# Graph attention: the closing sums of a block dealt out over five source tiles, the negated features one tile behind their low halves

## The chip, the cores and the metric

The kernel runs on one core of one Trainium2 chip. The metric is device microseconds of one execution. Three runs of the kernel before took 1197.7, 1198.29 and 1210.78 us; their median, 1198.29 us, is the time before.

## The reference, cut to what matters

A graph of 3125 nodes (64 features) and 100000 edges goes through four residual layers, each followed by a layer norm: ten rounds of normalized neighbour sums, an edge-feature layer with batch norm, two rounds of neighbour sums with two linear maps, and a four-headed graph attention. Only the last is touched here:

```python
logits = leaky_relu(a_src[src] + a_dst[dst], 0.2)        # per edge (self loops added), per head
ex     = exp(logits - seg_max[dst])
alpha  = ex / (segment_sum(ex, dst)[dst] + 1e-16)
out    = segment_sum(x[src] * alpha[:, :, None], dst).mean(heads) + bias
x      = layernorm(x + out)
```

## The kernel before, in words

Early stages turn the edge list into a dense count matrix `C` in SBUF (f16, 25 source tiles of 128 nodes by 3200 target columns) and run the first three layers as matmuls against it. In attention no exponential is taken per edge. Because the leaky ReLU has two slopes, an edge's weight is one of two products of a source factor and a target factor, and which one holds depends only on whether the logit is positive. So per head, source tile and target column the kernel needs a 0/1 step, times the count.

The stage runs over 4 heads (`h`), 5 blocks of 5 target tiles (`b`, 640 columns) and 25 source tiles (`t`); one (h, b, t) is called a unit here. In a unit:

- ScalarE (ACT, line 966) writes the step of 128x640 into `Mr`, a ring of 6 slots, with a sigmoid of a very steep slope. It waits until TensorE is done with the unit six earlier (`s_Mu`).
- VectorE (DVE, line 1587) multiplies it by the counts and signals `s_M`. For a few units per block (`STT`, line 1597) DVE makes the step itself.
- TensorE (PE) runs five matmuls `Mr` by `F` (line 2141, 260 columns: features for both slopes, each as a high and a low f16 half) and five matmuls of the plain counts by `FN` (line 2137, 130 columns: the negated features of the other slope). For some units (`SPLIT`) the plain matmuls are replaced by a complement that DVE makes (`Nr`, line 1550) and PE uses one unit later (line 2207). The plain matmuls of the first two target tiles of a block are sent ahead of the block ("lead").

Two kinds of work are threaded between the units on DVE and ACT by hand-written tests on `t`:

- **Features.** For each head and each group of 5 source tiles, PE makes `x` times the head's weight (`xw`), DVE scales it into `Vx` (`scaled`, line 1471), ACT rounds the high half into `F` (`high_f`, line 907; waits for `Vx`), DVE makes the low half (`low_f`, line 1487; waits for `s_fhi`) and, behind a wait on that, the negated copy `FN` (line 1489), which signals `s_F`. PE waits on `s_F` at the head's block 0: for the first three groups at once in heads 1 to 3, and ahead of the first unit of each later group. In head 0 all of this lies in block 0. For the later heads three groups are made in block 4 of the head before and two in block 0 of the head itself.
- **Closing sums.** At t = 4 of the next block ACT and DVE take a finished block from PSUM (lines 942 and 1496). At t = 5 `post` (lines 1502 to 1510) runs five DVE operations, each waiting for the one before: join the halves, denominator, reciprocal, product, add to `acc`. It signals `s_post`, which ACT waits for at t = 4 of the block after (`take`) and the first step of `final` waits for. In the last head `final` (lines 1518 to 1539) runs the layer norm of the block before in six steps at t = 8, 10, 12, 14, 16, 18, and signals `s_fin`, for which SP sends the rows out.

`c` counts DVE operations on a semaphore; `c.here()` is a wait of DVE for all that it has counted. SP's queue stores the target scores to DRAM (line 577) and then, in the branch of this path, waits for that store (`s_rowsout`) and loads each block's scores back, broadcast over partitions, one block ahead (line 604).

Of the kernel before, what the change touches and what calls it, by code (L numbers as in the profile page):

```python
# [4 lines left out]
ALU = mybir.AluOpType  # L5
# [7 lines left out]
P = 128  # L13
LO = 2048.0
# [24 lines left out]
def gnn_kernel(nc, x, dst, edges, We, be, W1, b1, gamma, beta, W2, b2, Wl, bl, Wr, br, Wg, att_s, att_d, bias_g, out):  # L39
    N, D = out.shape  # L40
# [15 lines left out]
    H = att_s.shape[1]  # L56
# [6 lines left out]
    XS = 256.0  # L63
    S1 = D + 1
# [7 lines left out]
    NG = 5  # L72
    NT = T // NG
# [25 lines left out]
    with ExitStack() as ctx:  # L99
# [102 lines left out]
        acc = xs  # L202
# [165 lines left out]
        def pairs_of(t0):  # L368

            return F[:, t0:t0 + NT, :].rearrange("p t (e l c) -> p (t e) l c", e=2, l=2)  # L370
# [141 lines left out]
        def _(sp):  # L512
# [62 lines left out]
                general_hop(kk, kk % 2)  # L575
            sp.wait_ge(s_minusrow, 1)
            sp.dma_start(minus_dram.rearrange("h (t p) -> (h t) p", p=P), minus_row[:]).then_inc(s_rowsout, 16)
            sp.wait_ge(s_flag3, 1)
            dense3 = sp.value_load(flag[0:1, 1:2], min_val=0, max_val=1)
            with sp.If(dense3 == 0):  # L580
# [13 lines left out]
                        sp.dma_start(g_raw[0:GE, :], edges[bass.ds(ch * GE, GE), :]).then_inc(g_load3, 16)  # L594
            with sp.Else():

                sp.wait_ge(s_rowsout, 16)
                for blk in range(1, H * NG):
                    if blk >= 2:
                        sp.wait_ge(s_M, (blk - 1) * T)  # L600
                    else:
                        sp.wait_ge(s_whl, 1)
                    b_ = blk % NG
                    sp.dma_start(nadS[blk % 2], minus_dram[blk // NG:blk // NG + 1, b_ * NG * P:(b_ + 1) * NG * P].to_broadcast([P, NG * P])).then_inc(s_nadl[blk % 2], 16)
# [114 lines left out]
        def _(act):  # L719
# [180 lines left out]
            def high_f(h, g):  # L900

                gi = h * NG + g
                t0 = g * NT
                act.wait_ge(s_vx, gi + 1)
                if h:
                    act.wait_ge(s_Mu, unit(h - 1, NG - 1, t0 + NT - 1) + 1)
                act.activation(pairs_of(t0)[:, :, 0, :], Vx[gi % 2].rearrange("p t e c -> p (t e) c"), ACT.Copy, scale=1.0 / LO).then_inc(s_fhi, 1)  # L907
# [26 lines left out]
            with act.If(dense3 == 1):  # L934

                def take(h, b):

                    act.wait_ge(s_Mu, unit(h, b, T - 1) + 1)
                    act.wait_ge(s_post, h * NG + b)
                    for j in range(NT):  # L940
                        t = b * NT + j
                        act.activation(r1[:, j], bank[:, BANKS[b][j], 0:2 * S1], ACT.Identity, scale=ex[:, 1, h, t:t + 1]).then_inc(s_c2, 1)

                for h in range(H):
                    for b in range(NG):
                        blk = h * NG + b
                        if blk:
                            act.wait_ge(s_nadl[blk % 2], 16 * ((blk + 1) // 2))
                        else:
                            act.wait_ge(s_nads, 1)  # L950
                        for t in range(T):
                            mi = unit(h, b, t)
                            if t == 4 and blk:
                                take((blk - 1) // NG, (blk - 1) % NG)
                            if blk == 0 and t in (1, 6, 11, 16):
                                high_f(0, (t + 4) // 5)
                            if blk and b == 0 and t in (9, 16):
                                high_f(h, 3 + t // 16)
                            if b == NG - 1 and h < H - 1 and t in (11, 16, 21):
                                high_f(h + 1, (t - 11) // 5)  # L960
                            if by_act(h, b, t):
                                if mi >= RB:
                                    act.wait_ge(s_Mu, mi - RB + 1)
                                    if unit_of(mi - RB) in APART:
                                        act.wait_ge(s_N, APART[unit_of(mi - RB)] + 1)
                                act.activation(Mr[:, mi % RB, :], nadS[blk % 2], ACT.Sigmoid, bias=steep[:, h, t:t + 1], scale=-STEEP / XS).then_inc(s_step, 1)  # L966
                act.activation(small[0:1, 63:64], onesP[0:1, :], ACT.Sqrt)
                act.wait_ge(s_post, H * NG - 1)
                for j in range(NT):
                    t = (NG - 1) * NT + j  # L970
                    act.wait_ge(s_Mu, unit(H - 1, NG - 1, T - LATE) + j + 1)
                    act.activation(r1[:, j], bank[:, BANKS[NG - 1][j], 0:2 * S1], ACT.Identity, scale=ex[:, 1, H - 1, t:t + 1]).then_inc(s_c2, 1)
                for part_, (a_, z_) in enumerate(((0, FRONT), (FRONT, NT))):
                    act.wait_ge(s_var, 3 * NB + part_ + 1)
                    act.activation(sd[:, a_:z_], mv[:, a_:z_, 1], ACT.Sqrt, bias=eps_c[:]).then_inc(s_sd, 1)
                act.wait_ge(s_rs, NB + 1)
                for j in range(FRONT):
                    t = (NG - 1) * NT + j
                    last = act.activation(acc[:, t, :], acc[:, t, :], ACT.Identity, bias=small[:, 40 + j:41 + j], scale=small[:, 32 + j:33 + j])
                last.then_inc(s_fin, 1)  # L980
# [11 lines left out]
        def _(v):  # L992
# [487 lines left out]
            with v.If(dense3 == 1):  # L1480

                def low_f(h, g):

                    gi = h * NG + g
                    t0 = g * NT
                    v.wait_ge(s_fhi, gi + 1)
                    c.add(v.scalar_tensor_tensor(pairs_of(t0)[:, :, 1, :], pairs_of(t0)[:, :, 0, :], -LO, Vx[gi % 2].rearrange("p t e c -> p (t e) c"), ALU.mult, ALU.add))  # L1487
                    c.here()
                    v.tensor_scalar(FN[:, t0:t0 + NT, :], F[:, t0:t0 + NT, 2 * S1:4 * S1], -1.0, None, ALU.mult).then_inc(s_F, 1)  # L1489

                def evicted(h, b):

# [2 lines left out]
                        v.wait_ge(s_c2, TURN[h, b, j] + 1)  # L1495
                        v.scalar_tensor_tensor(r1[:, j], bank[:, BANKS[b][j], 2 * S1:4 * S1], ex[:, 3, h, t:t + 1], r1[:, j], ALU.mult, ALU.add).then_inc(s_ring, 1)

                def post(h, b):

                    t0 = b * NT  # L1500
                    v.wait_ge(s_ring, TURN[h, b, NT - 1] + 1)
                    c.add(v.scalar_tensor_tensor(q, r1[:, :, S1:2 * S1], 1.0 / LO, r1[:, :, 0:S1], ALU.mult, ALU.add))
                    c.here()
                    c.add(v.tensor_scalar(rd[:], q[:, :, D], 1e-16 * XS, float(H), ALU.add, ALU.mult))
                    c.here()
                    c.add(v.reciprocal(rd[:], rd[:]))
                    c.here()
                    c.add(v.tensor_tensor(q[:, :, 0:D], q[:, :, 0:D], rd[:, :, None].to_broadcast([P, NT, D]), ALU.mult))
                    c.here()
                    v.tensor_tensor(acc[:, t0:t0 + NT, :], acc[:, t0:t0 + NT, :], q[:, :, 0:D], ALU.add).then_inc(s_post, 1)  # L1510

                def final(b, step):

# [36 lines left out]
                    v.tensor_tensor(Nr[ni % RN], Mr[:, unit(h, b, t) % RB, :], C[:, t, b * NT * P:(b + 1) * NT * P], ALU.subtract).then_inc(s_N, 1)  # L1550

                low_f(0, 0)
                scaled(0, 1)
                v.wait_ge(s_self, NB)
                for h in range(H):
                    for b in range(NG):
                        blk = h * NG + b
                        for t in range(T):
                            mi = unit(h, b, t)
                            if t == 4 and blk:  # L1560
                                evicted((blk - 1) // NG, (blk - 1) % NG)
                            if t == 5 and blk:
                                post((blk - 1) // NG, (blk - 1) % NG)
                            if blk == 0:
                                if t in (5, 10, 15):
                                    scaled(0, (t + 5) // 5)
                                elif t in (2, 7, 12, 17):
                                    low_f(0, (t + 3) // 5)
                            elif b == 0:
                                if t in (8, 15):  # L1570
                                    scaled(h, 2 + t // 7)
                                elif t in (11, 18):
                                    low_f(h, 2 + t // 9)
                            if b == NG - 2 and h < H - 1 and t in (10, 15):
                                scaled(h + 1, (t - 10) // 5)
                            if b == NG - 1 and h < H - 1:
                                if t == 14:
                                    scaled(h + 1, 2)
                                elif t in (12, 17, 22):
                                    low_f(h + 1, (t - 12) // 5)  # L1580
                            if h == 0 and b == 0 and t == 14:
                                c.add(v.tensor_tensor(acc[:], acc[:], biases[:, 2:3, :].to_broadcast([P, T, D]), ALU.add))
                            if h == H - 1 and b >= 1 and t in (8, 10, 12, 14, 16, 18):
                                final(b - 1, (t - 8) // 2)
                            if by_act(h, b, t):
                                v.wait_ge(s_step, steps(h, b, t))
                                v.tensor_tensor(Mr[:, mi % RB, :], Mr[:, mi % RB, :], C[:, t, b * NT * P:(b + 1) * NT * P], ALU.mult).then_inc(s_M, 1)  # L1587
# [699 lines left out]
```

## Time and profile before

| | us |
|---|---|
| median of the runs | 1198.29 |
| the profiled execution, its time | 1197.28 |
| its span, first to last instruction | 1195.4 |
| PE busy in the span | 1082.5 (91%) |
| DVE busy | 863.9 (72%) |
| ACT busy | 628.7 (53%) |
| line 2141, PE matmuls of steps by features | 321.2 |
| line 2137, PE matmuls of counts by negated features | 187.3 |
| line 1587, DVE products of steps and counts | 207.6 |

The page of the profile has the busy time of each engine, the span in 40 slices, the chain of work that ended last, and the costliest groups of instructions with the idle time before them. Attention fills the slices from the 26th on: there PE stands at 9 tenths or more, DVE and ACT at 9, and PE's granted clock at 9 tenths or more of full speed. Idle time is put down to what ended it.

### The profile page before, as it was taken

How to read it: one execution, taken by the hardware profiler on the slowest of the kernel's cores; microseconds unless marked ns; L12 is line 12 of the kernel's file. 1: busy time of each engine (PE TensorE's matmuls, PEld its weight loads, DVE VectorE, ACT ScalarE, POOL GpSimd, SP SyncE). 2: the span in 40 equal slices, each digit the busy share in tenths (PEclk: the TensorE clock that was granted, in tenths of full speed). 3: DMA queues.
4: the chain of work that ended last, by engine and by line, in shares of the span. 5: the costliest groups of instructions: out<-in, count | busy, mean ns of one | idle time of the engine just before them, and what ended most of it. 6: DMA issues, size and time to landing. Idle time of an engine off the chain costs nothing.

```text
span 1195.4 us, 38826 instructions
## 1 busy us (share of the span) xinstructions
PE 1082.5 (91%) x15999; PEld 997.2 (83%) x15999; DVE 863.9 (72%) x2311; ACT 628.7 (53%) x1172; POOL 59.6 (5%) x106
## 2 busy tenths in 40 slices
PE   4877777779999999999998999599999999999997
PEld 3766666669999999999973999489989988998996
DVE  5999999975444444444562544789999999999997
ACT  2777777730000000000111402579989999998997
POOL 1000000001111111111000011000000000000000
PEclk7899999989999999999999799699999999999999
DMA  5555555510000000000000000000000000000010
GB/s 80 69 78 77 72 74 73 71 39 3 2 3 2 3 2 3 2 2 3 2 2 1 2 2 2 15 12 13 24 12 24 13 24 13 24 13 20 16 29 14
DMA packets 135931, 28.04 MB, mean 23 GB/s; under 512 B 132609, under 2 KB 133093, under 8 KB 135778
## 3 DMA queue, kind: packets, MB, share of 16 engines
q1 hardware_dynamic: 132816, 25.25, 12.9%
q8 instruction: 116, 1.90, 0.7%
q10 hardware_dynamic: 2962, 0.58, 0.3%
q14 instruction: 37, 0.30, 0.1%
HBM read 24.97 MB, written 0.85 MB: 22 GB/s over the span
## 4 chain that ended last, share of the span: by engine, by line
PE 63%; DVE 12%; ACT 3%; issue 2%; ACTq 0%; POOL 0%; DVEq 0%
PE bank L2018 33%; PE bank L2141 13%; PE bank L2137 6%; DVE Mr L1587 4%; PE bank L1955 3%; PE bank L2207 2%; PE bank L1947 2%; ACT Mr L966 1%; DVE F L1487 1%; PE bank L1982 1%; PE bank L1939 1%; ACT F L907 1%; PE bank L2040 1%; DVE Mr L1597 1%; DVE FN L1489 0%
## 5 line engine op out<-in xcount | busy, mean ns | idle before, releaser
L2018 PE MATMUL bank<-GH,C 128*128 128x128 f16 x7100 | 397.7, 219 | 0.0
L2018 PEld LDWEIGHTS bank<-GH,C 128*128 128x128 f16 x7100 | 396.9, 98 | 0.1
L2141 PE MATMUL bank<-F,Mr 128*128 128x260 f16 (+1 forms) x2538 | 321.2, 261 | 10.0 <-DVE Mr L1587 8.7
L2141 PEld LDWEIGHTS bank<-F,Mr 128*128 128x128 f16 x2538 | 213.2, 98 | 33.7 <-DVE Mr L1587 11.0
L1587 DVE TENSOR_TENSOR Mr<-Mr,C 128x640 f16<-128x640 f16 x461 | 207.6, 485 | 25.4 <-ACT Mr L966 24.3
L814 ACT ACTIVATE plo<-bank 128x256 f32<-128x256 f32 (+1 forms) x84 | 30.1, 360 | 364.3 <-PE bank L2018 346.0
L2137 PE MATMUL bank<-FN,C 128*128 128x130 f16 x1945 | 187.3, 220 | 0.0
L1234 DVE TENSOR_TENSOR S<-bank,plo 128x256 f32<-128x256 f32 (+1 forms) x84 | 33.2, 395 | 212.9 <-ACT plo L814 212.8
L1810 PE MATMUL bank<-ohk,ohp 128*128 128x100 f16 (+3 forms) x1452 | 115.9, 216 | 69.6 <-ACT C L756 35.1
L966 ACT ACTIVATE Mr<-cold,eaT 128x640 f16<-128x640 f32 x231 | 172.4, 819 | 8.1 <-PE bank L2141 7.7
L966 ACT ACTIVATE Mr<-eaT 128x640 f16<-128x640 f32 x230 | 171.7, 818 | 7.3 <-PE bank L2141 7.0
L1810 PEld LDWEIGHTS bank<-ohk,ohp 128*128 128x128 f16 x1452 | 88.4, 101 | 79.2 <-ACT C L756 45.5
L2137 PEld LDWEIGHTS bank<-FN,C 128*128 128x128 f16 x1945 | 138.0, 98 | 4.9
L756 ACT ACTIVATE C<-bank 128x325 f32 (+1 forms) x242 | 111.0, 459 | 58.9 <-PE bank L1820 52.6
L1066 DVE TENSOR_TENSOR ohk<-iota_key,key 128x904 f16<-128x904 f16 (+7 forms) x264 | 106.5, 473 | 0.0
L1820 PEld LDWEIGHTS bank<-ohj,eahl 128*65 128x65 f16 x968 | 71.6, 117 | 11.1
L1825 PE MATMUL bank<-C,spare 128*128 (+1 forms) x242 | 79.1, 328 | 0.2 <-ACT C L756 0.2
L1068 DVE TENSOR_TENSOR ohp<-iota_p,pl 128x2048 f16<-128x2048 f16 (+1 forms) x66 | 75.2, 1139 | 0.0
L1820 PE MATMUL bank<-ohj,eahl 128*65 128x6 f16 x968 | 66.9, 177 | 0.0
L646 POOL TENSOR_TENSOR xc<-xs,cold 128x256 f32<-128x256 f32 (+1 forms) x63 | 40.3, 645 | 520.0 <-DVE V L1250 267.2
L1121 DVE SCALAR_TENSOR_TENSOR GH<-GH,V 128x256 f16<-128x256 f16 (+1 forms) x84 | 47.1, 561 | 2.9
L1056 DVE TENSOR_TENSOR raw<-raw,eahl 128x768 f32<-128x768 f32 (+1 forms) x44 | 39.4, 895 | 3.0 <-ACT eahl L745 3.0
(271 smaller groups left out, 984.4 us busy)
## 6 DMA issues: line engine op xcount, KB each, us to landing
raw<-in_edges_dram SPq DMA_DIRECT2D x237, 68.0 KB, 2.5
cold<-minus_dram SPq DMA_DIRECT2D x10, 320.0 KB, 3.3
eaT<-minus_dram SPq DMA_DIRECT2D x9, 320.0 KB, 3.5
xs<-in_x_dram SPq DMA_DIRECT2D x1, 800.0 KB, 4.4
out_dram<-xs SPq DMA_DIRECT2D x4, 160.0 KB
raw<-in_edges_dram ACTq DMA_DIRECT2D x5, 68.0 KB, 3.2
dsts<-in_dst_dram SPq DMA_DIRECT2D x1, 240.0 KB
dsts<-in_dst_dram ACTq DMA_DIRECT2D x1, 180.0 KB
```

The source lines that it names most:

```text
L756: act.activation(C[:, :, bass.ds(wi * W, W)], pk[w % RING][:, 0:KEY].rearrange("p (j t) -> p t j", t=T), ACT.Copy).then_inc(s_evict, 1)
L966: act.activation(Mr[:, mi % RB, :], nadS[blk % 2], ACT.Sigmoid, bias=steep[:, h, t:t + 1], scale=-STEEP / XS).then_inc(s_step, 1)
L1066: v.tensor_tensor(ohk[:, o:o + n, OK[k]:OK[k + 1]].rearrange("p w (n e) -> p w n e", e=2), pairs(iota_key[:, OK[k]:OK[k + 1]], n), key2[:, ...
L1068: v.tensor_tensor(ohp[:, o:o + n].rearrange("p w k (n e) -> p (w k) n e", e=2), pairs(iota_p[:], n * K), pl2[:, par, w0:w1_].rearrange("p ...
L1121: last = v.scalar_tensor_tensor(GH[:, par, t0:t0 + n, D:2 * D], GH[:, par, t0:t0 + n, 0:D], -LO, src, ALU.mult, ALU.add)
L1587: v.tensor_tensor(Mr[:, mi % RB, :], Mr[:, mi % RB, :], C[:, t, b * NT * P:(b + 1) * NT * P], ALU.mult).then_inc(s_M, 1)
L1810: pe.matmul(pk[r][:, T * j0:T * j1], ohp[:, o, k], ohk[:, o, a_:a_ + T * (j1 - j0)], start=q_ == 0, stop=q_ == len(PART) - 1)
L1820: last = pe.matmul(pea[par][0:65, w * W + j0:w * W + j1], eahl[:, ch, :], ohj[:, par, j0:j1, ch], start=False, stop=w == WG - 1 and k == K ...
L1825: return pe.matmul(pdeg[:, 0:KEY].rearrange("p (t j) -> p t j", j=W), ident16, C[:, :, bass.ds(wi * W, W)], start=False, stop=stop)
L2018: last = pe.matmul(bank[:, b, jj * 2 * D:(jj + 1) * 2 * D], C[:, t, (t0 + jj) * P:(t0 + jj + 1) * P], GH[:, par, t, :], start=t == 0 and j ...
L2137: pe.matmul(bank[:, k, 2 * S1:4 * S1], C[:, t, t_ * P:(t_ + 1) * P], FN[:, t, :], start=start, stop=False)
L2141: return pe.matmul(bank[:, k, a_:z_], Mr[:, mi % RB, j * P:(j + 1) * P], F[:, t, a_:z_], start=start, stop=t == T - 1)
```

## The change

SP's wait for its store of the target scores is moved ahead of the read of the branch flag. ACT's `high_f` calls of block 0 are moved to later `t`. On DVE, `FN` leaves `low_f` and becomes `plain_f`, called one source tile later, with its 650 elements walked in the order (half, tile, column), rows of 65, where they were walked (tile, column), rows of 130. `post` is cut into five calls, one at each of t = 5 to 9. Some `low_f` calls and all steps of `final` are moved to later `t`. PE's code is untouched.

```diff
@@ sync
             sp.dma_start(minus_dram..., minus_row[:]).then_inc(s_rowsout, 16)
+            sp.wait_ge(s_rowsout, 16)
             sp.wait_ge(s_flag3, 1)
...
-                sp.wait_ge(s_rowsout, 16)
@@ scalar
-                            if blk == 0 and t in (1, 6, 11, 16):
+                            if blk == 0 and t in (1, 8, 13, 18):
                                 high_f(0, (t + 4) // 5)
-                            if blk and b == 0 and t in (9, 16):
-                                high_f(h, 3 + t // 16)
+                            if blk and b == 0 and t in (11, 18):
+                                high_f(h, 3 + t // 18)
@@ vector
                     c.add(v.scalar_tensor_tensor(pairs_of(t0)[:, :, 1, :], ..., -LO, Vx[...], ALU.mult, ALU.add))
+
+                def plain_f(g):
+
+                    t0 = g * NT
                     c.here()
-                    v.tensor_scalar(FN[:, t0:t0 + NT, :], F[:, t0:t0 + NT, 2 * S1:4 * S1], -1.0, None, ALU.mult).then_inc(s_F, 1)
+                    v.tensor_scalar(FN[:, t0:t0 + NT, :].rearrange("p t (l c) -> p l t c", l=2), F[:, t0:t0 + NT, 2 * S1:4 * S1].rearrange("p t (l c) -> p l t c", l=2), -1.0, None, ALU.mult).then_inc(s_F, 1)
...
-                def post(h, b):
+                def post(h, b, step):
...
                 low_f(0, 0)
+                plain_f(0)
                 scaled(0, 1)
...
-                            if t == 5 and blk:
-                                post((blk - 1) // NG, (blk - 1) % NG)
+                            if 5 <= t < 10 and blk:
+                                post((blk - 1) // NG, (blk - 1) % NG, t - 5)
                             if blk == 0:
                                 if t in (5, 10, 15):
                                     scaled(0, (t + 5) // 5)
-                                elif t in (2, 7, 12, 17):
+                                elif t in (2, 8, 13, 18):
                                     low_f(0, (t + 3) // 5)
+                                elif t in (3, 9, 14, 19):
+                                    plain_f((t + 2) // 5)
                             elif b == 0:
                                 if t in (8, 15):
                                     scaled(h, 2 + t // 7)
-                                elif t in (11, 18):
+                                elif t in (12, 18):
                                     low_f(h, 2 + t // 9)
+                                elif t in (13, 19):
+                                    plain_f(2 + t // 9)
...
                                 elif t in (12, 17, 22):
                                     low_f(h + 1, (t - 12) // 5)
+                                elif t in (13, 18, 23):
+                                    plain_f((t - 13) // 5)
...
-                            if h == H - 1 and b >= 1 and t in (8, 10, 12, 14, 16, 18):
-                                final(b - 1, (t - 8) // 2)
+                            if h == H - 1 and b >= 1 and t in (10, 12, 14, 16, 18, 20):
+                                final(b - 1, (t - 10) // 2)
```

## Rows read from the trace of the kernel before

**Rows 1.** Waits from 770 us on: us in total, times, longest us.

```profile
DVE Mr L1587 <- ACT Mr L966: 24.3, 62, 1.1
...
PE bank L2141 <- DVE Mr L1587: 8.7, 16, 2.7
```

**Rows 2.** Windows: stretch, its us, busy us (instructions) by engine, PEclk, DMA share, GB/s.

```profile
800.30:880.00 79.70, 79.08 (x1049) 73.35 (x1047) 74.03 (x176) 74.62 (x115) 0.00 (x0) 1.00 0.06 15
1104.00:1124.00 20.00, 19.86 (x254) 18.24 (x253) 19.11 (x68) 19.00 (x30) 0.00 (x0) 1.00 0.05 18
```

**Rows 3.** Timeline, head 0, block 0: start us, us, engine, line, form, [idle before].

```profile
787.27 1.82 DVE L1582 TENSOR_TENSOR xs<-xs,cold 128x1600 f32<-128x1600 f32 x1
787.86 0.72 PE L2141 MATMUL bank<-F,Mr 128*128 128x260 f16 x5
...
793.99 0.73 PE L2141 MATMUL bank<-F,Mr 128*128 128x260 f16 x5 [0.66 <-DVE Mr L1587]
...
796.51 0.72 PE L2141 MATMUL bank<-F,Mr 128*128 128x260 f16 x5
```

**Rows 4.** Timeline, head 0, block 4: DVE's second feature group, then PE's units.

```profile
871.83 0.83 DVE L1487 SCALAR_TENSOR_TENSOR F<-F,eaT 128x650 f16<-128x650 f16 x1
872.69 0.49 DVE L1489 TENSOR_SCALAR FN<-F 128x650 f16<-128x650 f16 x1
873.10 1.29 DVE L1587 TENSOR_TENSOR Mr<-Mr,C 128x640 f16<-128x640 f16 x3
...
871.84 0.72 PE L2141 MATMUL bank<-F,Mr 128*128 128x260 f16 x5
872.56 0.72 PE L2141 MATMUL bank<-F,Mr 128*128 128x260 f16 x5
873.64 0.73 PE L2141 MATMUL bank<-F,Mr 128*128 128x260 f16 x5 [0.19 <-DVE Mr L1587]
876.39 0.72 PE L2141 MATMUL bank<-F,Mr 128*128 128x260 f16 x5
877.71 0.73 PE L2141 MATMUL bank<-F,Mr 128*128 128x260 f16 x5 [0.43 <-DVE Mr L1587]
```

**Rows 5.** Timeline, head 1, block 0, around its last feature group.

```profile
891.64 0.83 DVE L1471 TENSOR_TENSOR Vx<-bank,ex 128x650 f32<-128x650 f32 x1
892.39 0.48 DVE L1587 TENSOR_TENSOR Mr<-Mr,C 128x640 f16<-128x640 f16 x1
892.51 0.76 ACT L907 ACTIVATE F<-Vx 128x650 f16<-128x650 f32 x1 [0.99 <-DVE Vx L1471]
893.37 0.72 PE L2141 MATMUL bank<-F,Mr 128*128 128x260 f16 x5
894.56 0.73 PE L2141 MATMUL bank<-F,Mr 128*128 128x260 f16 x5 [0.19 <-DVE Mr L1587]
896.95 0.73 PE L2141 MATMUL bank<-F,Mr 128*128 128x260 f16 x5 [0.54 <-DVE Mr L1587]
```

**Rows 6.** Timeline, head 3, block 1: DVE's closing sums.

```profile
1107.92 0.49 DVE L1502 SCALAR_TENSOR_TENSOR wts<-r 128x325 f32<-128x325 f32 x1
1108.45 0.17 DVE L1504 TENSOR_SCALAR rd<-wts 128x5 f32<-128x5 f32 x1
...
1109.40 0.49 DVE L1510 TENSOR_TENSOR xs<-xs,wts 128x320 f32<-128x320 f32 x1
```

**Rows 7.** Timeline, the last block: PE's weight loads for its last unit.

```profile
1183.72 0.56 PEld L2141 LDWEIGHTS bank<-F,Mr 128*128 128x128 f16 x6 [0.30 <-DVE Mr L1587]
```

**Rows 8.** Groups by line and form from 770 us on: count, busy us, mean ns, idle before.

```profile
L1489 DVE TENSOR_SCALAR FN<-F 128x650 f16<-128x650 f16 x20 | 9.9, 493 | 0.7
L1487 DVE SCALAR_TENSOR_TENSOR F<-F,eaT 128x650 f16<-128x650 f16 x10 | 8.3, 829 | 0.8 <-ACT F L907 0.8
```

**Rows 9.** Timeline, SP's queue: the store of the scores, the first load back.

```profile
769.18 0.34 SPq L577 DMA_DIRECT2D minus_dram<-minus_row  x1
770.73 0.35 SPq L604 DMA_DIRECT2D cold<-minus_dram  x1
```

More of the change, by code:

```diff
@@ L1496, in evicted @@
                         v.scalar_tensor_tensor(r1[:, j], bank[:, BANKS[b][j], 2 * S1:4 * S1], ex[:, 3, h, t:t + 1], r1[:, j], ALU.mult, ALU.add).then_inc(s_ring, 1)
-                def post(h, b):
+                def post(h, b, step):
                     t0 = b * NT
[L1501 to L1510, printed above, removed]
+                    if step == 0:
+                        v.wait_ge(s_ring, TURN[h, b, NT - 1] + 1)
+                        c.add(v.scalar_tensor_tensor(q, r1[:, :, S1:2 * S1], 1.0 / LO, r1[:, :, 0:S1], ALU.mult, ALU.add))
+                    elif step == 1:
+                        c.here()
+                        c.add(v.tensor_scalar(rd[:], q[:, :, D], 1e-16 * XS, float(H), ALU.add, ALU.mult))
+                    elif step == 2:
+                        c.here()
+                        c.add(v.reciprocal(rd[:], rd[:]))
+                    elif step == 3:
+                        c.here()
+                        c.add(v.tensor_tensor(q[:, :, 0:D], q[:, :, 0:D], rd[:, :, None].to_broadcast([P, NT, D]), ALU.mult))
+                    else:
+                        c.here()
+                        v.tensor_tensor(acc[:, t0:t0 + NT, :], acc[:, t0:t0 + NT, :], q[:, :, 0:D], ALU.add).then_inc(s_post, 1)
                 def final(b, step):
```

## The prediction

> **What bounds the kernel now.** I read the windows first, to find where attention is held; then the waits of that stretch by engine; then the timeline of PE, DVE and ACT around each wait; then the groups for durations. In the stretch from 800 to 880 us PE is busy for 79.08 of 79.70 us at full granted clock, with DVE and ACT at 74 [rows 2]: three engines nearly level, PE the bound. What DVE can still give back is PE's wait for a step times counts. These waits are 16, 8.7 us in all [rows 1]. The longest, 2.7 us, is the first unit of the stage, which this change leaves alone; the others are three in the first block and four at each of the three changes of head. That DVE in its turn waits 62 times for ACT, 24.3 us in all, says that DVE is not always the late one.
>
> The idle time that a row gives in brackets understates the loss, because a matmul's end is modelled; I count from start to start. In block 0 the units from 793.99 to 796.51 us come every 0.84 us, but four units take 6.13 us from 787.86 to 793.99 [rows 3]: 2.77 us lost. In block 4 of head 0 the pace is 0.72 us; two units come 0.36 and 0.60 us later than that (873.64 and 877.71) [rows 4]. In block 0 of head 1 the pace is 0.84 again; the two starts at 894.56 and 896.95 us lose 0.35 and, over two units, 0.71 us [rows 5]. The last two patterns stand three times.
>
> **What causes them.** In block 4 DVE makes a low half and, chained to it, the negated copy, 0.86 + 0.41 us, in front of one product for which PE is already waiting [rows 4]. In block 0 of head 1 ACT asks for the high half's input at t = 16 and stands 0.99 us until DVE has scaled it at t = 15; the steps of t = 16 and 17 queue behind that [rows 5]. In block 0 of head 0 both happen, with the 1.82 us addition of the biases besides [rows 3].
>
> **The change, part by part.**
> *Negated copy one tile later.* Twenty copies [rows 8] move behind one product. The chain gap goes: from a chained 0.83 us operation to the next start it takes 0.86 us [rows 4], from an unchained one 0.75 [rows 5], so 0.11 each. In block 4 the product of t = 17 then comes 0.41 + 2 x 0.11 = 0.63 us sooner against 0.36 lost, and that of t = 22 comes 0.41 + 3 x 0.11 = 0.74 us sooner against 0.60. The products right behind the moved copies, t = 18 and 23, still gain 0.22 and 0.33. So 0.96 us goes in each of three blocks: **2.9 us**. The margin left there is some 0.1 us at t = 23.
> *PE's wait on that copy* costs nothing by order alone: each copy is issued ahead of the product of the tile before the one where PE asks (3, 9, 14, 19 against 5, 10, 15, 20; 23 against the next block), and PE cannot pass that product.
> *High halves later on ACT.* At t = 18 in place of 16 two more steps go ahead of the wait; the scaled input is done at 891.64 + 0.83 = 892.47 us, about when ACT has finished them, so the 0.99 us stand and PE's 0.35 + 0.71 go: 1.06 us three times, **3.2 us**. Behind the high half on ACT queues the step of the same tile, and DVE's low half waits for it; but the product behind that low half needs that step too, so the worst new wait is the high half's own 0.76 us, in front of a product that comes those 0.99 us and its copy's 0.41 us earlier than now.
> *Block 0.* The high halves at 8, 13, 18 come after their inputs (5, 10, 15), so ACT's stands go; the low half at 8, and the copies at 9, 14, 19, split the bursts. The bias addition stays at t = 14, now behind a copy of 0.41 us and ahead of the scaling, but two of ACT's stands lie ahead of it, and if each is worth the 0.99 us of [rows 5], DVE reaches it 2 us earlier, more than the longest burst in front of one product that it is part of now. The four late units come back: **2.8 us**. If only the split worked, and ACT's stands stayed, it would be about half of that.
> *Closing sums over five tiles.* A 0.49 us operation in the chain takes 0.53 us to the next start [rows 6], one outside it 0.41 [rows 4]: 0.12 us for each of four waits, 0.48 us of DVE per block, 19 times. In the blocks where PE has no stall this is worth nothing: the lead matmuls hide DVE there, and if DVE were late by the same amount PE would lose it one for one. In the last head, where the norm of the block before also lies on DVE, PE stands 0.14 us per block by the window [rows 2]; that is the lower bound, 0.48 the upper. I take 0.3, between them, three times: **0.9 us**. In the last block PE's weight load for the last unit waits 0.30 us for DVE [rows 7]: DVE ends that block. Between 0.30 and 0.48 I take **0.4 us**. The signal of the sums comes four tiles later; ACT asks for it nineteen tiles after that, and the norm's first step one tile after, on DVE itself.
> *Norm two tiles later.* No product comes later than before, since only work in front of it was taken away. The rows of a block go to SP's queue about two tiles, 1.7 us, later; the last such store has the drain behind 1183.72 us as cover.
> *SP's moved wait.* From store to first load 1.55 us pass [rows 9], the wait among them; reading the flag now follows the wait. The load can come earlier by nothing and later by at most that stretch again; block 1 uses it after 796.51 us [rows 3], 25 us on. Nothing of POOL's queue is passed.
> *The walk by halves.* No row has an f16 copy in rows of 65. From below a copy cannot take less than the 0.17 us of a five-element operation [rows 6]; from above stands 0.83 us, the low half over the same 650 elements [rows 8]. I keep 0.493 us, the same operation's row. At 0.17 the stage's first unit gains 0.32 us and the margins grow, little more; at 0.83 each copy is 0.34 us longer, which undoes the gain in block 4 and adds 0.34 us at the first unit.
>
> Of the walk two pages of the Trainium skill speak. The one titled VectorE: DVE Perf Modes, section "Mode 2×_1P", wants 4-byte alignment for two 16-bit values per read; the second half starts 130 bytes into the row, so by it that half would lose the pairing. That would put the copy toward 0.83 us, a result of its own (second case below). The page Vector Engine (DVE) Microarchitecture Reference, section 5.1, says that alignment makes no difference, and that an even outermost count lets both read ports work as well; the walk turns a count of 5 into 2. By that I estimate 0.17 + (0.49 - 0.17) / 2 = 0.33 us, and the sum would be lower by 0.2 us. That today's copy runs at two elements per step agrees with both: (493 - 172) / (829 - 172) is 0.49.
>
> **Sum.** 2.9 + 3.2 + 2.8 + 0.9 + 0.4 = 10.2 us. I take 1.0 off, a tenth, because margins of 0.1 us will not all hold: 9.2. The profiled execution took 1197.28 us, 1.0 under the median: 1188.1 in its terms, **1189** as a median. From the bounds (0.17 and 0.48 - 0.3 three times below, half of block 0 above) this case runs from 1187 to 1191.5.
>
> **Rivals.**
> 1. *Block 4 stays late*: the copy by halves takes 0.83 us, or a margin of 0.1 us fails. Lost are 2.9, 0.3 at the first unit and some of the rest: 1193, from 1191.5 to 1195. For it: the odd second half, the thin margin. Against: today's copy does pair.
> 2. *The stalls only move*: ACT's 24.3 us of waits [rows 1] come from the six-slot ring, and a DVE that is early waits for ACT. Then no more than the tail comes back: 1196 to 1198. Against it: at each PE wait shown DVE or ACT is held by a burst or by the order of asking, not by the ring. The change not doing what it says (each split step still paying its wait) is a part of this: it would lose the 0.9 and 0.4 and put the time at 1190.
> 3. *Slower*: the copy by halves becomes one of the longest DVE operations. Ten copies are exposed (nine in block 4, one at the first unit), so each 0.1 us costs 1 us, and beyond 0.49 + 0.92 = 1.4 us it eats the whole gain. At the 1.82 us of the longest row [rows 3], which moves two and a half times as many elements, the time is 1189 + 10 x 1.33 = 1202, more with the other ten. Only that nothing shows this form speaks for it.
>
> **Numbers.** Forecast 0.63, first rival 0.20, second 0.13, third 0.04. The range from 1186 to 1196 takes in the first two cases and the edge of the third; about 0.16 lies outside. Two per cent is 24 us, about what a measurement of this kernel can tell from no change; all PE waits of the stage together are less, so faster by that has 0.01, slower 0.02, within 0.97.
>
> **What would show it.** In the changed profile PE's waits for the product should fall from 16 to the first and a few, 8.7 us to about 3; the starts of block 0's late units should be 0.84 us apart and those of block 4 0.72; ACT should no longer stand near 1 us for the scaled input at the head's block 0; the closing sums should stand singly between products, the next start 0.41 us on. The copy's mean decides between the forecast and the first and third rivals. The forecast is wrong if PE's waits stay as many, or if they go and the stage (first unit to last) is not some 9 us shorter.

## The result, and the profile after

The changed kernel takes 1190.86 us (median of 20 runs, 1188.21 to 1206.2) against 1198.1 us (20 runs, 1196.28 to 1211.55): a ratio of 0.9947, 95% interval 0.9924 to 0.9969. The interval is 9.1 to 3.7 us of gain; 1189 was forecast. Six of the changed kernel's runs and three of the kernel before stand 9 to 15 us above their median, in the changed kernel at a mean granted clock of 0.941 to 0.952 where its other runs have 0.965 to 0.970; they pull the ratio toward 1, and the two medians alone give 0.9940. The profiled execution took 1190.22 us with a span of 1188.3, where the one before took 1197.28 and 1195.4, so the two spans differ by 7.1 us, and the rest of this section places those.

Line numbers move with the new code: the products' matmuls are L2157 (L2141 before), the lead's L2153 (L2137), DVE's products L1603 and L1613 (L1587, L1597), the negated copy L1493 (L1489), the complement of a tile's products L1559, DVE's eviction of the lead's bank L1500, the five closing sums L1507 to L1519.

The waits of the changed kernel from 760 us on come first (us in total, times, longest), against [rows 1]:

```profile
DVE Mr L1603 <- ACT Mr L966: 24.9, 76, 1.1
...
PE bank L2157 <- DVE Mr L1603: 2.6, 1, 2.6
...
ACT F L907 <- DVE Vx L1471: 1.3, 1, 1.3
...
PE bank L2157 <- DVE Mr L1613: 1.2, 3, 0.4
...
PE bank L2153 <- DVE r L1500: 0.9, 3, 0.3
...
ACT F L907 <- DVE eaT L1471: 0.4, 1, 0.4
```

Of 16 waits of PE for a product on the first product line one is left, the first unit's. Two kinds stand there that [rows 1] did not have, three times each: one for the other product line (L1613, the step that DVE makes itself) and one for a bank (L1500). DVE waits for ACT as long as ever, 24.9 us.

Next, the timeline of the changed kernel: block 0 of head 0 (PE, against [rows 3]); block 4 of head 0 (DVE, then PE, against [rows 4]); block 0 of head 1 (against [rows 5]).

```profile
787.98 0.72 PE L2157 MATMUL bank<-F,Mr 128*128 128x260 f16 x5
788.81 0.72 PE L2157 MATMUL bank<-F,Mr 128*128 128x260 f16 x5
...
791.33 0.72 PE L2157 MATMUL bank<-F,Mr 128*128 128x260 f16 x5
...
868.77 0.83 DVE L1487 SCALAR_TENSOR_TENSOR F<-F,eaT 128x650 f16<-128x650 f16 x1
869.51 0.49 DVE L1603 TENSOR_TENSOR Mr<-Mr,C 128x640 f16<-128x640 f16 x1
869.91 0.33 DVE L1493 TENSOR_SCALAR FN<-F 128x650 f16<-128x650 f16 x1
...
869.07 0.72 PE L2157 MATMUL bank<-F,Mr 128*128 128x260 f16 x5
869.79 0.72 PE L2157 MATMUL bank<-F,Mr 128*128 128x260 f16 x5
...
887.93 0.83 DVE L1471 TENSOR_TENSOR Vx<-bank,ex 128x650 f32<-128x650 f32 x1
888.83 0.75 ACT L907 ACTIVATE F<-Vx 128x650 f16<-128x650 f32 x1
```

The late units of block 0 come every 0.83 to 0.84 us, and those around the copy in block 4 every 0.72. A product now stands between the low half and its copy, and starts 0.74 us after the low half, where the chained copy had started 0.86 us after it. ACT takes the scaled input at 888.83 without a wait, where 0.99 us stood before it; DVE had it ready at 887.93 + 0.83 = 888.76, so the margin is 0.07 us.

The new waits: first the lead from head 0 to head 1, then the last head's block 1 (DVE from the start of its eviction to the step that it makes itself, PE's late unit), the starts of two successive leads there, DVE's longest wait in the last block, the weight load of the last unit, and SP's queue:

```profile
875.98 0.92 PE L2153 MATMUL bank<-FN,C 128*128 128x130 f16 x13
876.71 0.48 DVE L1559 TENSOR_TENSOR spare<-Mr,C 128x640 f16<-128x640 f16 x1
877.11 1.39 DVE L1500 SCALAR_TENSOR_TENSOR r<-bank,ex,r 128x130 f32<-128x130 f32 x5
877.52 0.93 PE L2153 MATMUL bank<-FN,C 128*128 128x130 f16 x13 [0.28 <-DVE r L1500]
...
1098.08 0.35 DVE L1500 SCALAR_TENSOR_TENSOR r<-bank,ex,r 128x130 f32<-128x130 f32 x1 [0.39 <-ACT r L942]
...
1099.84 0.49 DVE L1603 TENSOR_TENSOR Mr<-Mr,C 128x640 f16<-128x640 f16 x1 [0.36 <-ACT Mr L966]
1100.25 0.49 DVE L1507 SCALAR_TENSOR_TENSOR wts<-r 128x325 f32<-128x325 f32 x1
...
1101.75 0.49 DVE L1603 TENSOR_TENSOR Mr<-Mr,C 128x640 f16<-128x640 f16 x1 [0.54 <-ACT Mr L966]
...
1113.18 0.88 DVE L1613 SCALAR_TENSOR_TENSOR Mr<-eaT,asad,C 128x640 f16<-128x640 f32 x1
...
1114.12 0.73 PE L2157 MATMUL bank<-F,Mr 128*128 128x260 f16 x5 [0.41 <-DVE Mr L1613]
...
1097.48 1.32 PE L2153 MATMUL bank<-FN,C 128*128 128x130 f16 x20
...
1117.71 1.32 PE L2153 MATMUL bank<-FN,C 128*128 128x130 f16 x20
...
1162.68 0.49 DVE L1603 TENSOR_TENSOR Mr<-Mr,C 128x640 f16<-128x640 f16 x1 [0.77 <-ACT Mr L966]
...
1176.65 0.56 PEld L2157 LDWEIGHTS bank<-F,Mr 128*128 128x128 f16 x6 [0.31 <-DVE Mr L1603]
...
769.62 0.34 SPq L577 DMA_DIRECT2D minus_dram<-minus_row  x1
772.12 0.35 SPq L604 DMA_DIRECT2D cold<-minus_dram  x1
```

Each such pair of lead starts is 20.23 us apart (1097.48 to 1117.71). Measured in that way, from the start of one block's lead to the next, every block has a length that doesn't depend on how late the layers ahead of attention were. A block's stretch runs to the start of the next block's lead; the first begins with the stage's first unit and the last ends with the span. All stretches come from PE's timeline in one execution of each kernel:

| stretch, us | before | after | times | change in all |
|---|---|---|---|---|
| head 0, block 0 | 27.85 | 24.89 | 1 | -2.96 |
| blocks 1 and 2, heads 0 to 2 | 18.87 | 18.82 | 6 | -0.3 |
| block 3 | 19.88 | 19.89 | 3 | 0 |
| block 4, heads 0 to 2 | 21.69 | 20.71 | 3 | -2.93 |
| block 0, heads 1 to 3 | 22.27 | 21.67 | 3 | -1.78 |
| last head, blocks 1 to 3 | 20.13 | 20.23 | 3 | +0.3 |
| last head, block 4, to the end | 29.84 | 30.13 | 1 | +0.29 |
| first unit's start | 772.57 | 772.85 | 1 | +0.28 |

They sum to 7.1 us, or 7.4 without the last row, from the first unit to the end. The first unit starts 0.28 us later because the work ahead of attention was 0.44 us later in this execution (SP's store at 769.62 against 769.18 in [rows 9]), and the copy ahead of that unit is 0.16 us shorter. So two of the forecast terms came back in full, a third only in part, and the last head, where a gain was forecast, lost.

### The profile page after: what moved, and what is told of

Its sections match the earlier page's. It is cut to its first block, busy times and chain, and to the rows that moved or that the text cites. A ratio compares the mean times of both kernels' runs of the same rounds, so it can differ in the third digit from the quotient of the medians.

```text
span 1188.3 us, 38826 instructions
## 1 busy us (share of the span) xinstructions
PE 1079.5 (91%) x15999; PEld 996.9 (84%) x15999; DVE 855.7 (72%) x2311; ACT 629.9 (53%) x1172; POOL 59.8 (5%) x106
## 3 DMA queue, kind: packets, MB, share of 16 engines
q1 hardware_dynamic: 132816, 25.25, 12.9%
## 4 chain that ended last, share of the span: by engine, by line
PE 70%; DVE 7%; ACT 1%; issue 1%; ACTq 0%; POOL 0%; DVEq 0%
PE bank L2034 33%; PE bank L2157 17%; PE bank L2153 8%; PE bank L1971 3%; PE bank L2223 2%; DVE Mr L1603 2%; PE bank L1963 2%; PE bank L1955 1%; PE bank L1998 1%; PE bank L2119 1%; ACT Mr L966 1%; PE bank L2056 1%; PE bank L2076 0%; DVE ohk L1066 0%; DVE xs L1548 0%
## 5 line engine op out<-in xcount | busy, mean ns | idle before, releaser
L2157 PE MATMUL bank<-F,Mr 128*128 128x260 f16 (+1 forms) x2538 | 321.1, 261 | 4.7 <-DVE Mr L1603 2.6
L2157 PEld LDWEIGHTS bank<-F,Mr 128*128 128x128 f16 x2538 | 214.5, 98 | 25.0 <-issue 2.7
L1603 DVE TENSOR_TENSOR Mr<-Mr,C 128x640 f16<-128x640 f16 x461 | 213.4, 487 | 27.8 <-ACT Mr L966 24.9
L2153 PE MATMUL bank<-FN,C 128*128 128x130 f16 x1945 | 187.3, 220 | 0.9 <-DVE r L1500 0.9
L2153 PEld LDWEIGHTS bank<-FN,C 128*128 128x128 f16 x1945 | 137.9, 98 | 6.3 <-DVE r L1500 1.7
```

Source lines behind the costliest of these rows:

```text
L2153: pe.matmul(bank[:, k, 2 * S1:4 * S1], C[:, t, t_ * P:(t_ + 1) * P], FN[:, t, :], start=start, stop=False)
L2157: return pe.matmul(bank[:, k, a_:z_], Mr[:, mi % RB, j * P:(j + 1) * P], F[:, t, a_:z_], start=start, stop=t == T - 1)
```

## The experiments

Four questions were open. Did **order** give the gain of blocks 0 and 4, or the shorter copy? Does ACT's **place of asking** matter by itself? What took away part of the gain in block 0 of heads 1 to 3? Why did the last head lose? Single executions are compared by the stretches of the table, since their whole times also hold the layers ahead of attention, which differ from one execution to the next. All but the last kernel have one execution each; blocks that an edit doesn't touch agree within 0.03 us among the executions of the changed kernel and its variants, apart from block 0 of head 0, which the clock moves (last section), and the last block, where the same code took 30.13 to 30.29 us. In b1, b2 and b3 lines from L1574 on have a number higher by one.

**a1: the changed kernel with the copy walked by tiles again.**

```diff
-v.tensor_scalar(FN[:, t0:t0 + NT, :].rearrange("p t (l c) -> p l t c", l=2), F[...].rearrange(...), -1.0, ...)
+v.tensor_scalar(FN[:, t0:t0 + NT, :], F[:, t0:t0 + NT, 2 * S1:4 * S1], -1.0, ...)
```

> The changed kernel, but the negated copy is walked by tiles (rows of 130) as before; it still stands one tile behind its low half. Theory (order): the stalls went because of where operations stand, not because the copy got shorter (336 ns against 493). Then the copy's mean returns to about 493 ns, the first unit of the stage comes 0.16 us later, and the intervals between the lead starts of the blocks stay within 0.2 us of the changed kernel's: block 0 of head 0 24.9 (first unit to next lead), block 4 of heads 0 to 2 20.7, block 0 of heads 1 to 3 21.7 us. In all 0.2 to 0.8 us longer than the changed kernel. Rival (walk): the shorter copy is what keeps block 4 free of waits; then block 4 goes back toward 21.7 us, 0.6 to 1.0 us in each of three heads, 2 to 3 us in all.

The copy's group by line and form, first of the changed kernel, then of a1 (count, busy us, mean ns, idle before):

```profile
L1493 DVE TENSOR_SCALAR FN<-F 128x650 f16<-128x650 f16 x20 | 6.7, 336 | 0.0
```

```profile
L1493 DVE TENSOR_SCALAR FN<-F 128x650 f16<-128x650 f16 x20 | 9.8, 490 | 0.0
```

Block 4 took 20.99 us (20.71), block 0 of heads 1 to 3 21.52 (21.67, so a little less), all others as in the changed kernel. The walk saves 154 ns per copy and 0.28 us of block 4, which is more than the 0.2 that the expectation allowed and less than half of the rival's 0.6 to 1.0.

**b4: the kernel before, with nothing but the walk by halves.**

```diff
-v.tensor_scalar(FN[:, t0:t0 + NT, :], F[:, t0:t0 + NT, 2 * S1:4 * S1], -1.0, ...)
+v.tensor_scalar(FN[:, t0:t0 + NT, :].rearrange("p t (l c) -> p l t c", l=2), F[...].rearrange(...), -1.0, ...)
```

> The kernel before, with one edit: the negated copy is walked by halves where it stands, behind its low half. Its mean falls to about 336 ns, 0.16 us less at each of 20 places. Theory (order): the bursts and ACT's order of asking stay, so little comes back: the first unit 0.16 us earlier, block 4 of heads 0 to 2 21.3 to 21.5 us where they take 21.69, block 0 of heads 1 to 3 22.0 to 22.2 where they take 22.27, block 0 of head 0 27.4 to 27.7 where it takes 27.85: 1 to 2 us in all. Rival (walk): the shorter copy does most of what the whole change does, 4 us or more.

Its copy's group:

```profile
L1489 DVE TENSOR_SCALAR FN<-F 128x650 f16<-128x650 f16 x20 | 6.8, 341 | 0.7
```

Block 4 took 21.21 us, slightly better than expected, and block 0 of heads 1 to 3 22.11. With a1 this makes a square for block 4: before 21.69, walk alone 21.21, order alone 20.99, both 20.71. Order alone gives 0.70 of the 0.98 us, the walk alone 0.48. They overlap; that they do because both shorten the same burst is our reading. Block 0 of head 0 took 26.93 us, less than expected, but most of that is the clock (last section), which rose 2.9 us after the first unit here and 5.4 us after it in the kernel before: its late units still lose 2.6 us, against 2.77.

**a4: the changed kernel with ACT's high halves at their old places.**

```diff
-if blk == 0 and t in (1, 8, 13, 18):
+if blk == 0 and t in (1, 6, 11, 16):
...
-if blk and b == 0 and t in (11, 18):
-    high_f(h, 3 + t // 18)
+if blk and b == 0 and t in (9, 16):
+    high_f(h, 3 + t // 16)
```

> The changed kernel, but ACT's high halves stand where they stood before (t = 6, 11, 16 in head 0's block 0; 9 and 16 in block 0 of the later heads); all of DVE's changes stay. Theory (order of asking): ACT then stands near 1 us for the scaled input again, and the two late units of block 0 of heads 1 to 3 come back in part: these blocks take 22.2 to 22.7 us where they take 21.67, and block 0 of head 0 takes 26 to 27.5 where it takes 24.9; 3 to 5 us in all. Rival (DVE's split): the waits went because DVE's bursts were split, and ACT runs far enough ahead; then less than 1 us in all comes back.

The waits of a4, then its timeline at the last feature group of head 1's block 0 (all of this execution is some 10 us later than the others, from the layers ahead):

```profile
ACT F L907 <- DVE eaT L1471: 6.5, 5, 2.7
ACT F L907 <- DVE Vx L1471: 6.4, 5, 2.1
```

```profile
901.62 0.76 ACT L907 ACTIVATE F<-Vx 128x650 f16<-128x650 f32 x1 [1.02 <-DVE Vx L1471]
```

ACT waits 12.9 us for the scaled input, where 1.7 us are left in the changed kernel; the 0.99 us of [rows 5] stands again as 1.02. Block 0 of heads 1 to 3 took 22.23 us (21.67), block 0 of head 0 27.25. The fair comparison for the latter is with runs in which the clock rose as early, 2.9 us after the first unit: b1 with 23.87, and b4 with 26.93. So with ACT asking early, the later copies give nothing back in block 0 of head 0; the 3.4 us hang on the place of asking. Whether ACT's later places alone, without the moved copies, would do as much was not run.

**a3: the changed kernel with the complement at t = 4, not 2, in a head's block 0.**

```diff
-SPLIT = ((2, 13, 20, 22), ...
+SPLIT = ((4, 13, 20, 22), ...
```

> The changed kernel, but in block 0 of heads 1 to 3 the first complement is that of source tile 4 in place of 2, so DVE makes it after the eviction of the block before and not right ahead of it. Theory (eviction): PE's second lead tile waits for its bank, which DVE gives back only behind this complement (0.40 us); then the wait of 0.28 us at that lead goes, the time from the first to the second lead start falls from 1.54 to about 1.14 us, block 0 of heads 1 to 3 from 21.67 to about 21.3 us, 1.1 to 1.3 us in all. Rival (ACT): the eviction waits for ACT, which is busy without a gap at the end of block 4 and takes the bank first; then the lead interval stays at 1.45 to 1.54 us and nothing is gained.

a3's timeline at the lead from head 0 to head 1:

```profile
874.72 0.92 PE L2153 MATMUL bank<-FN,C 128*128 128x130 f16 x13
875.44 1.39 DVE L1500 SCALAR_TENSOR_TENSOR r<-bank,ex,r 128x130 f32<-128x130 f32 x5
875.84 0.93 PE L2153 MATMUL bank<-FN,C 128*128 128x130 f16 x13
```

The second tile of the lead starts 1.12 us after the first (1.54 in the changed kernel), its wait is gone, and block 0 of heads 1 to 3 takes 21.25 us: 0.42 less, three times. So the bank was the new wait: in the changed kernel DVE evicts it behind the complement of t = 2 (876.71, then 877.11), and PE arrives before DVE is through.

**a2: the norm's last steps drawn forward to t = 18.** This tests the first theory of the last head, that the norm's last step (1.20 us), now at t = 20, collides with the products due there.

```diff
-t in (10, 12, 14, 16, 18, 20): final(b - 1, (t - 10) // 2)
+t in (10, 11, 12, 14, 16, 18): final(b - 1, (10, 11, 12, 14, 16, 18).index(t))
```

> The changed kernel, but the six steps of the last head's norm stand at t = 10, 11, 12, 14, 16, 18, so that the last step (five operations, 1.1 us) does not stand right ahead of the step that DVE makes itself at t = 20. Theory (burst): the new wait of 0.41 us at t = 20 in blocks 1 to 3 of the last head comes from these two standing together; apart, the wait falls to 0.1 us or goes, these blocks take 19.8 to 19.95 us where they take 20.23, and the last block to the end 0.2 to 0.4 us less than 30.13: 1.0 to 1.5 us in all. Rival (load): DVE has too much to do in these blocks wherever it stands; then the wait moves to t = 18 and the blocks stay at 20.1 to 20.25 us.

a2's timeline in the last head's block 1:

```profile
1109.59 1.20 DVE L1548 TENSOR_SCALAR xs<-xs,mv,eaT 128x64 f32<-128x64 f32 x5
...
1111.25 1.01 PE L2157 MATMUL bank<-F,Mr 128*128 128x260 f16 x10 [0.22 <-DVE Mr L1603]
```

The wait moved with the step, to t = 18, and the blocks stayed at 20.23 us. The burst theory fell: the place of the step sets where PE waits, not what the block loses. That left the rival, that DVE is late through the whole stretch; the next two runs ask whether it is so because it stood idle early in the block.

**b2: the changed kernel with the sums in one piece at t = 5**, which by itself adds the chain's waits back.

```diff
-if 5 <= t < 10 and blk:
-    post((blk - 1) // NG, (blk - 1) % NG, t - 5)
+if t == 5 and blk:
+    for step in range(5):
+        post((blk - 1) // NG, (blk - 1) % NG, step)
```

> The changed kernel, but the five closing operations run in one piece at t = 5 in every block, each waiting for the one before, as before the change. That gives DVE back its four chained waits, 0.48 us more work per block. Theory (hiding place): in the last head this costs nothing or even gains, since the piece runs while DVE would wait for ACT: blocks 1 to 3 take 20.1 to 20.15 us, as in the kernel before, where they take 20.23 with less work on DVE. Elsewhere at most 0.1 us per block changes. Rival (load): with 0.48 us more on DVE these blocks take 20.4 to 20.7 us.

**b1: the sums of the last head at t = 4, 5, 6, 6, 7 in place of 5 to 9.**

```diff
-if 5 <= t < 10 and blk:
-    post((blk - 1) // NG, (blk - 1) % NG, t - 5)
+for step in (((4, 0), (5, 1), (6, 2), (6, 3), (7, 4)) if h == H - 1 and b
+             else ((5, 0), (6, 1), (7, 2), (8, 3), (9, 4))) if blk else ():
+    if step[0] == t:
+        post((blk - 1) // NG, (blk - 1) % NG, step[1])
```

> The changed kernel, but in blocks 1 to 4 of the last head the five closing operations stand at t = 4, 5, 6, 6, 7 in place of 5 to 9. Theory (hiding place): before the change the closing sums ran at t = 5 in a time in which DVE had to wait for ACT's step of t = 6 anyway; dealt out to 9 they are done after that step has come, in the stretch where DVE has no idle time up to t = 20, so they cost what they last. Brought forward again, some 0.4 us of them go back into the waits of 0.36 and 0.54 us at t = 4 and 6, and blocks 1 to 3 of the last head take 19.8 to 19.95 us where they take 20.23, the last block 0.2 to 0.4 less than 30.13. Rival (load): DVE's work per block counts, wherever it stands; then these blocks stay within 0.1 us of 20.23, as they did when the norm's steps were moved.

DVE in the last head's block 1, from the start of its eviction to the step that it makes itself at t = 20: first in the kernel before, then in b2 (with PE's late unit), then in b1 (with ACT's step of t = 6):

```profile
1105.76 0.35 DVE L1496 SCALAR_TENSOR_TENSOR r<-bank,ex,r 128x130 f32<-128x130 f32 x1
...
1120.77 0.88 DVE L1597 SCALAR_TENSOR_TENSOR Mr<-eaT,asad,C 128x640 f16<-128x640 f32 x1
```

```profile
1098.83 0.35 DVE L1500 SCALAR_TENSOR_TENSOR r<-bank,ex,r 128x130 f32<-128x130 f32 x1 [0.39 <-ACT r L942]
...
1100.58 0.49 DVE L1604 TENSOR_TENSOR Mr<-Mr,C 128x640 f16<-128x640 f16 x1 [0.36 <-ACT Mr L966]
...
1113.83 0.88 DVE L1614 SCALAR_TENSOR_TENSOR Mr<-eaT,asad,C 128x640 f16<-128x640 f32 x1
...
1114.77 0.73 PE L2158 MATMUL bank<-F,Mr 128*128 128x260 f16 x5 [0.31 <-DVE Mr L1614]
```

```profile
1097.51 0.35 DVE L1500 SCALAR_TENSOR_TENSOR r<-bank,ex,r 128x130 f32<-128x130 f32 x1 [0.39 <-ACT r L942]
...
1100.61 0.49 DVE L1516 TENSOR_TENSOR wts<-wts,rd 128x320 f32<-128x320 f32 x1
1101.18 0.49 DVE L1604 TENSOR_TENSOR Mr<-Mr,C 128x640 f16<-128x640 f16 x1
...
1112.30 0.88 DVE L1614 SCALAR_TENSOR_TENSOR Mr<-eaT,asad,C 128x640 f16<-128x640 f32 x1
...
1100.32 0.83 ACT L966 ACTIVATE Mr<-eaT 128x640 f16<-128x640 f32 x1 [0.37 <-PE bank L2158]
```

This stretch holds the same operations in all four kernels. DVE takes 15.01 us for it in the kernel before, 15.10 in the changed kernel, 15.00 in b2 and 14.79 in b1, and PE's block follows one for one: 20.13, 20.23, 20.13 and 19.91 us. Inside it the changed kernel's DVE waits 0.36 + 0.54 = 0.90 us for ACT's steps and has none of the four links of the chain; b2 waits 0.36 and has the links, which by the 0.12 us of the forecast are 0.48: 0.84 in all. b1 has one link and its waits for ACT are small, not gone: 1101.18 is 0.57 us behind the sum ahead of it, in place of 0.41, because ACT's step ends at 1100.32 + 0.83 = 1101.15. PE's late unit waits 0.41 us in the changed kernel, 0.31 in b2, and has no wait listed in b1. The sums in one piece, with more waits of their own, beat the sums dealt out, because the piece lies where DVE would have waited for ACT anyway. Everywhere else the dealt-out sums are a small gain: blocks 1 and 2 take 18.88 us in b2 and 18.82 in the changed kernel. The last block takes 30.13 us in the changed kernel, 29.88 in b2, and 29.95 in b1, a gain a little smaller than expected. Up to PE's last matmul it takes 21.56, 21.30 and 21.22 us (21.29 in the kernel before), so b1's repair is whole there, and the rest of its stretch, the drain, took 0.16 us more in that execution.

**b3: both repairs at once**, b1's sums and a3's complement.

```diff
-SPLIT = ((2, 13, 20, 22), ...
+SPLIT = ((4, 13, 20, 22), ...
...
+for step in (((4, 0), (5, 1), (6, 2), (6, 3), (7, 4)) if h == H - 1 and b else ...
```

> The changed kernel with both edits: the closing operations of the last head at t = 4, 5, 6, 6, 7, and the first complement of block 0 of heads 1 to 3 at source tile 4. Theory: the two add up, since they touch different blocks: 1.2 us of the second as measured alone, and 1.0 to 1.5 us of the first; 2.2 to 2.7 us less than the changed kernel, about 1188.4 us as a median, ratio to the kernel before 0.991 to 0.993. Rival: only the second counts, 1189.6 us.

b3 takes 1187.36 us (11 runs) against 1197.31 for the kernel before, run beside it (16 runs): a ratio of 0.9928, 95% interval 0.9908 to 0.9949. Its stretches add up as the parts did, 21.25 us for block 0 of heads 1 to 3 and 19.92 for the last head's blocks. It beats both kernels: against the changed kernel's median it is 3.5 us less, though those two were not run side by side; each against the kernel before that ran with it, it gains 9.95 us and the changed kernel 7.24, so 2.7 us of difference, at the upper end of what was expected. From 770 us on, one wait of PE's products and leads for DVE is left in it, the first unit's (weight loads still wait):

```profile
PE bank L2158 <- DVE Mr L1604: 2.6, 1, 2.6
```

## Why the prediction was right, and where not

The likeliest case held, both in its time and in its main mechanism. The sum was 2.1 us too large (9.2 against 7.1 between the profiled spans), and only two of its five terms have their size. There is luck in that it was no more: the terms come to 10.2 us, and the tenth was taken off for thin margins, which held in block 4 with the shorter copy, and it made up for part of what was lost in other places. The upper end of the likeliest case, 1191.5, does not come out of the bounds named for it either: half of block 0 above 1189 is 1190.4, just under the 1190.86 measured. By the forecast's own signs, the stage should have been some 9 us shorter and is 7.4, and PE's waits for a product should have fallen to about 3 us and are 3.8, with 0.9 for the bank.

- **Block 4, 2.9 us forecast, 2.93 measured.** The copy moved behind one product, and the pace is 0.72 us throughout. The walk's share was not in the sum; a1 shows that without it 0.28 us per block would have stayed. So the order alone fell short (0.70 of the 0.96 us in a1), and the shorter copy made it good.
- **Block 0 of head 0, 2.8 forecast, 2.96 measured.** The reason was right too as far as ACT goes: a4 shows that without its later place of asking nothing is gained. The aside that the split alone would give half fell: with ACT early it gave nothing.
- **Block 0 of heads 1 to 3, 3.2 forecast, 1.78 measured.** The term itself is sound: 0.60 + 0.42 = 1.02 us per head with a3's repair, against 1.06. The step that failed is what was left out of it. The forecast asked what is late next for the products on DVE and ACT, not for PE's lead. That the lead comes sooner once block 4 is quicker is our reading; its second tile then waits for a bank that DVE frees behind a complement (0.28 us in the rows, 0.42 in the stretch).
- **Closing sums in the last head, 0.9 forecast, a loss of 0.3 measured; last block, 0.4 forecast, a loss of 0.29.** The step that failed is "0.12 us for each of four waits, 0.48 us of DVE per block": the links do go, but that time was booked as DVE's gain, as if DVE's waits for ACT would stay. That PE loses one for one what DVE loses held (15.01 to 15.10 us on DVE, 20.13 to 20.23 on PE). Steps 2 to 4 of the sums left the time in which DVE waits for ACT's products and went into the stretch without idle time (b1, b2), and DVE's waits for ACT grew by 0.54 us, more than the 0.48 saved. In the last block they grew from 0.27 to 0.28 + 0.77 us, and 0.78 less 0.48 is 0.30, the loss there. The row from which the last block's 0.4 us was taken, the last unit's weight load [rows 7], was misread: its wait is 0.30 or 0.31 us in every run, b1 among them, and stands as long at the weight loads of the units ahead of it, so it is the pace of DVE's products (0.40 us from one to the next, 0.10 us the load) and no measure of what DVE could give back. The size was not out of reach: b1's and b3's blocks 1 to 3 are 0.21 to 0.22 us under the kernel before, though not their last block.
- **"No product comes later than before, since only work in front of it was taken away"** failed as well. Moving the norm's last step to t = 20 put it in front of the product of that tile, which waits 0.41 us. By a2 this is not a cost of its own: with the step moved back the wait shows two tiles sooner, and the block takes the same 20.23 us.
- **Nothing was forecast for blocks 1 and 2**; six of them gained 0.05 us each, by b2 from the sums.
- **SP's moved wait** cost nothing, as forecast: from store to first load 2.50 us pass in place of 1.55, and no wait that was found follows from it; no run tried it by itself.
- **The walk.** 336 ns stands where 493 ns was kept; the 0.16 us at the first unit, which the sum did not hold, came. The Trainium skill's page Vector Engine (DVE) Microarchitecture Reference, section 5.1, says that an even outermost count lets both read ports work and that alignment makes no difference; the forecast's estimate under it was 0.33 us, and the trace agrees (336 ns). By the 4-byte alignment that the Trainium skill's page VectorE: DVE Perf Modes, section "Mode 2×_1P", asks for, the second half would have lost its pairing, which the forecast put toward 0.83 us; a1 (490 ns) and b4 (341 ns) show a shorter copy instead. Only this walk was tried, so the runs show that it is shorter and not why.

Of the rivals, the first fell with the 336 ns and block 4's pace, and the third with the same number. The second was right about one thing: DVE's waits for ACT did not shrink (24.3 to 24.9 us, 62 to 76 times). They were not PE's waits, though, and the stalls went all the same, except in the last head, where a wait for ACT is what decides.

## What to carry to other kernels

An idle stretch of an engine that waits for another is a place to hide work: before work is dealt out or deferred, see whether it leaves such a stretch for one without idle time, because then its own saved waits count for less than the cover lost. Where two engines serve each other in fixed order, move the one's request behind the other's supply before anything is made shorter. And when a stall is taken away, ask what the freed engine wants next in a resource that nobody was late for, such as a bank to be evicted, and not only in the queue in which the stall was.

## What the runs showed of the hardware

The granted clock of TensorE is 0.50 (1.2 GHz) when attention begins and rises to 1.00 (2.4 GHz) at a moment that differs between executions. Windows of the changed kernel, then of b1 (stretch, its us, busy us and instructions by engine, clock, DMA share, GB/s):

```profile
777.00:778.00 1.00, 1.00 (x9) 0.82 (x7) 0.94 (x2) 1.00 (x2) 0.00 (x0) 0.50 0.00 0
778.00:779.00 1.00, 1.00 (x12) 0.91 (x11) 1.00 (x3) 0.77 (x2) 0.00 (x0) 0.94 0.00 0
```

```profile
776.00:777.00 1.00, 1.00 (x16) 0.67 (x15) 1.00 (x3) 1.00 (x2) 0.00 (x0) 0.85 0.00 0
777.00:778.00 1.00, 1.00 (x19) 0.93 (x15) 0.88 (x3) 1.00 (x3) 0.00 (x0) 1.00 0.00 0
```

In the changed kernel it rises at about 778.1 us, 5.3 us after the first unit (772.85); in b1 at about 776.3, 2.9 us after its first unit (773.37). Their code is the same up to there, and block 0 of head 0 takes 24.89 and 23.87 us. Over all ten profiled executions it rose 2.9 us after the first unit in three (a4, b1, b4) and 5.3 to 5.6 us after it in seven. So one execution's stretch of that block carries about 1 us that belongs to no edit; what sets the moment was not tried.

A one-source f16 copy of 650 elements takes 336 ns when it is walked as two halves and 493 when it is walked as five rows, with the same elements on both sides. That this is no effect of the new place shows in b4, where the copy stands where it stood and takes 341 ns.
